# A state-space scan kernel: most of the step sizes' last additions and products moved from VectorE's step stage into the scan on GpSimd

## The chip, the cores and the metric

One core of a Trainium2 chip runs the whole program in one launch. The metric is the device time of one execution in microseconds (us), lower is better. The engines are TensorE (PE in the profile; its weight loads are PEld), VectorE (DVE), ScalarE (ACT), GpSimd (POOL) and SyncE (SP), which issues the DMAs. Each engine runs its own list of instructions in order and meets the others through semaphores.

## The reference, cut to what matters

The model is four small layers on an image of 2 x 32 x 32 tokens with 32 channels. The change lies in the first one, a selective scan over 8 x 8 windows in four directions (64 inner channels, 16 states):

```python
x_dbl = jnp.einsum('bkdl,kcd->bkcl', xs, x_proj_w)
dts, Bs, Cs = jnp.split(x_dbl, [DT_RANK, DT_RANK + D_STATE], axis=2)
dts = jnp.einsum('bkrl,kdr->bkdl', dts, dt_projs_w)
dts = jax.nn.softplus(dts + dt_projs_b[None, :, :, None])
...
def step(h, inp):
    u, dt, Bl, Cl = inp
    dA = jnp.exp(dt[..., None] * A)
    h = h * dA + (dt * u)[..., None] * Bl[:, :, None, :]
    y = jnp.einsum('bkdn,bkn->bkd', h, Cl)
    return (h, y)
```

What follows (the directions put back in order and added, a layer norm, a gate, an output projection, and then the layers with two recurrences of 1,024 steps, the experts and the attention) is computed as before and is not touched.

## The kernel before

The four directions are held as two pairs: `k` is the pair, the 128 partitions are 2 directions x 64 channels, and the free axis is 16 windows x 128 positions = 2,048 columns. So `step` (the step sizes dt), `drive` (dt times u) and `seqf` (u) are each 128 x 2 x 2,048 in f32.

The work is cut into blocks. At a block's end every engine waits for all the others. Around the change there are three:

- The token stage (lines 343 to 410) turns the convolved image into tokens and these into the four scan orders. ScalarE only copies every second pair of windows there.
- The step stage (lines 413 to 507) computes softplus(v) as max(v, 0) + ln(1 + exp(-|v|)) with a small correction of what the f32 addition 1 + exp loses. It goes by 8 chunks of 512 columns. TensorE makes v (line 432), ScalarE makes |v|, max(v, 0) (`above`) and the exponential (lines 446 to 449), VectorE makes the correction and adds it to `above` (lines 466, 473, 481) and cuts the B and C projections into three bf16 parts (lines 470 to 484). ScalarE then takes the 8 logarithms (line 457). At the end VectorE puts `step` together for 1,024 columns at a time, log minus `ln_one` plus `above` (line 495; `ln_one` is the logarithm of 1 as the engine computes it), four times, and makes the first two products `drive` = `step` x `seqf` (line 489). When the first logarithm is there, TensorE multiplies a constant tile 16 times for nothing (`keep_streaming`, line 95). A line of the profile with L95 is always such filling.
- The scan (lines 557 to 776) has 64 units `u`: four groups of 1,024 columns (`u // 16`: pair 0 first half, pair 0 second half, pair 1 first half, pair 1 second half), and in each 16 states. For a unit TensorE spreads B over the partitions into PSUM (`p_bb`, line 587) and C (`p_cb`, line 593), ScalarE makes the decays `d_a` = exp(step x A) (line 659) and copies C to SBUF (`cb`, line 665), VectorE multiplies `drive` with B (line 712) and runs the recurrence with one scan instruction into `hs` (line 723), GpSimd multiplies `hs` with C into `hc` (line 776), and TensorE adds `hc` over the states into `p_y` (line 562, eight products of 128 columns). In each fourth unit (`u % 4 == 3`) GpSimd makes the product with B instead of VectorE (`d_bu`, line 771), from a copy that ScalarE makes (line 670) of a spread by TensorE (line 615), issued three units ahead at `u % 4 == 0`.

`hs`, `cb` and `hc` are rings of three, so the scan of unit u waits for the GpSimd product of unit u - 3 (`hc`), and TensorE's list at unit u has `p_bb(u)`, `p_cb(u)`, the sum of unit u - 3, and only then `p_bb(u + 1)`. The order of everything is written out by hand. GpSimd makes the other two `drive` products in the scan, at units 2 and 18 (line 767).

## Time and profile before

| | us |
|---|---|
| median of 3 runs | 990.17 (988.23 to 991.03) |
| the profiled execution | 990.42 |
| its span, first to last instruction | 988.6 |
| step stage, first to last work | about 36.6 to 67.1 |
| scan, first work to last scan instruction's end | about 67.4 to 276.2 |

The timeline rows below give a start, a duration and then engine, line and operation, `out<-in`, shapes and a count; in brackets stands how long the engine had been idle and what ended that. Rows that run together (x2) have one duration for the whole. Where operations overlap in their pipeline, the step from one start to the next is a little shorter than a duration. In the rows of windows each engine has its busy time in that stretch with the number of instructions, and then come the granted TensorE clock (1.00 is 2.4 GHz, 0.50 is 1.2 GHz), the busy share of the DMA engines and GB/s.

### The profile page before, as it was taken

The numbers are of one execution on the slowest core, as the hardware profiler recorded it, in microseconds if no ns is written. First come the engines' busy times: TensorE is split into PE (matmuls) and PEld (weight loads), VectorE is DVE, ScalarE is ACT, GpSimd is POOL, SyncE is SP. The second block draws the span as 40 slices with busy tenths as digits, with TensorE's granted clock in tenths as the row PEclk, the third lists the DMA queues.
The fourth block names the chain that finished last, engine by engine and source line by source line (L and its number), as shares of the span: only waits on it lengthen the run. The fifth ranks groups of instructions, "written<-read, shape, count | busy, mean of one in ns | idle before, by whom it ended". The sixth has DMA issues, their size and how long they took to land. (4 is left out here: it accounts for less than half of the span.)

```text
span 988.6 us, 15415 instructions
## 1 busy us (share of the span) xinstructions
PE 905.6 (92%) x6234; PEld 517.4 (52%) x6234; DVE 417.7 (42%) x715; ACT 446.4 (45%) x1491; POOL 230.8 (23%) x140
## 2 busy tenths in 40 slices
PE   7848888888989988899999999999999999999986
PEld 4416667667764444344444444445555544554543
DVE  4599999999966654600000000002005400302653
ACT  4667777777635443233333333333333333334542
POOL 3209999899820000110000000000000000000410
PEclk9968999999999997999999999999999999999887
DMA  3020000000000000200000000000000000000000
GB/s 80 15 51 1 1 1 2 1 1 1 1 1 6 2 24 11 80 1 1 1 1 1 1 1 2 1 1 1 1 1 1 1 1 1 1 1 2 1 24 11
DMA packets 10320, 8.30 MB, mean 8 GB/s; under 512 B 7346, under 2 KB 8610, under 8 KB 10152
## 3 DMA queue, kind: packets, MB, share of 16 engines
q1 hardware_dynamic: 10248, 7.31, 3.0%
q8 instruction: 49, 0.80, 0.4%
q14 instruction: 23, 0.19, 0.1%
HBM read 5.47 MB, written 0.26 MB: 6 GB/s over the span
## 5 line engine op out<-in xcount | busy, mean ns | idle before, releaser
L895 PE MATMUL L2p_z<-stream 128*128 128x512 bf16 x943 | 366.8, 390 | 0.0
L937 ACT ACTIVATE L2yx<-L2p_z 32x2 f32<-32x2 f32 x1024 | 165.3, 161 | 323.0 <-PE L2p_z L914 323.0
L914 PEld LDWEIGHTS L2p_z<-L2yx,L2v 64*32 64x32 f32 x2048 | 137.6, 104 | 224.7 <-ACT L2yx L937 218.5
L914 PE MATMUL L2p_z<-L2yx,L2v 64*32 64x2 f32 x2048 | 225.5, 178 | 1.0 <-PEq L811 0.9
L776 POOL TENSOR_TENSOR hc<-hs,cb 128x1024 f32<-128x1024 f32 x64 | 149.7, 2360 | 11.6 <-DVE hs L723 11.5
L562 PEld LDWEIGHTS p_y<-ident,hc 128*128 128x128 f32 x1024 | 125.1, 193 | 10.3 <-POOL hc L776 1.1
L1602 DVE COPY xn<-L2yx 32x512 f32<-32x512 f32 (+1 forms) x2 | 0.8, 384 | 302.7 <-ACT L2yx L937 302.7
L562 PE MATMUL p_y<-ident,hc 128*128 128x128 f32 x1024 | 125.7, 277 | 0.0
L1602 POOL COPY xn<-L2yx 32x128 f32<-32x128 f32 x1 | 0.3, 284 | 484.0 <-SPq L1945 484.0
L723 DVE TENSOR_TENSOR_SCAN hs<-d_a,p_bb 128x1024 f32<-128x1024 f32 x48 | 109.8, 2287 | 6.6 <-ACT d_a L659 0.5
L895 PEld LDWEIGHTS L2p_z<-stream 128*128 128x128 bf16 x943 | 90.1, 96 | 15.1
L665 ACT ACTIVATE cb<-p_cb 128x1024 f32<-128x1024 f32 x64 | 65.3, 1020 | 10.8 <-PE p_cb L593 10.3
L659 ACT ACTIVATE d_a<-step,decay 128x1016 f32<-128x1016 f32 x48 | 54.6, 1138 | 19.7 <-DVE hs L723 12.8
L712 DVE TENSOR_TENSOR p_bb<-drive,p_bb 128x1024 f32<-128x1024 f32 x48 | 58.1, 1209 | 2.3 <-PE p_bb L587 2.2
L593 PE MATMUL p_cb<-c_parts,pick 96*128 96x512 bf16 x128 | 40.0, 395 | 12.3 <-ACT d_bu L670 10.5
L587 PE MATMUL p_bb<-b_parts,pick 96*128 96x512 bf16 x96 | 30.0, 395 | 13.1 <-DVE hs L723 7.2
L771 POOL TENSOR_TENSOR d_bu<-drive,d_bu 128x1024 f32<-128x1024 f32 x16 | 37.9, 2368 | 8.5 <-ACT d_bu L670 8.5
L723 DVE TENSOR_TENSOR_SCAN hs<-p_bb,d_bu 128x1024 f32<-128x1024 f32 x16 | 36.3, 2266 | 0.7 <-ACT p_bb L659 0.7
L593 PEld LDWEIGHTS p_cb<-c_parts,pick 96*128 96x128 bf16 x128 | 10.8, 99 | 31.0 <-ACT d_bu L670 18.8
L670 ACT ACTIVATE d_bu<-p_cb 128x1024 f32<-128x1024 f32 x16 | 16.4, 1024 | 18.8 <-PE p_cb L615 18.8
L1011 ACT ACTIVATE L0yx<-L0p_z 32x64 f32<-32x64 f32 x96 | 15.5, 209 | 14.3 <-PE L0p_z L988 14.3
L95 PE MATMUL L0p_fill<-stream 128*128 128x512 bf16 x56 | 20.6, 388 | 0.0
(513 smaller groups left out, 883.0 us busy)
## 6 DMA issues: line engine op xcount, KB each, us to landing
y_l<-in_pick SPq DMA_DIRECT2D x1, 768.0 KB
b_parts<-part SPq DMA_DIRECT2D x6, 128.0 KB, 2.3
c_parts<-part SPq DMA_DIRECT2D x6, 128.0 KB, 2.3
pos<-in_pos SPq DMA_DIRECT2D x1, 512.0 KB, 3.6
ao<-in_at_o SPq DMA_DIRECT2D x1, 512.0 KB, 4.1
L1w<-in_L_w SPq DMA_DIRECT2D x1, 297.0 KB
L3w<-in_L_w SPq DMA_DIRECT2D x1, 297.0 KB
x_tok<-in_x SPq DMA_DIRECT2D x2, 128.0 KB, 3.0
```

What stands on the lines that cost most here:

```text
L562: last = pe.matmul(p_y[:, j], hc[:, v % RING, j * L:(j + 1) * L], ident[:], start=False, stop=(v % NS == NS - 1 and j % 4 == 3))
L587: last = pe.matmul(p_bb[:, u % 2, h * BANK:(h + 1) * BANK], pick[:, n], b_parts[:, k, c], start=True, stop=True)
L593: last = pe.matmul(p_cb[:, h * BANK:(h + 1) * BANK], pick[:, n], c_parts[:, k, c], start=True, stop=True)
L659: act.activation(dst[:, :, 1:L], src[:, :, 1:L], ACT.Exp, scale=decay[:, k, n:n + 1]).then_inc(sig["d_a"], 1)
L665: act.activation(cb[:, u % RING], p_cb[:], ACT.Copy).then_inc(sig["p_cb_read"], 1)
L712: dve.tensor_tensor(p_bb[:, u % 2], drive[:, k, c0:c0 + UC], p_bb[:, u % 2], ALU.mult).then_inc(sig["d_bu"], 1)
L723: dve.tensor_tensor_scan(hs[:, u % RING], decays, inputs, 0.0, ALU.mult, ALU.add).then_inc(sig["scanned"], 1)
L771: pool.tensor_tensor(d_bu_of(u), drive[:, k, c0:c0 + UC], d_bu_of(u), ALU.mult).then_inc(sig["d_bu_pool"], 1)
L776: pool.tensor_tensor(hc[:, u % RING], hs[:, u % RING], cb[:, u % RING], ALU.mult).then_inc(sig["hc"], 1)
L895: pe.matmul(p_z[:, 1, 0:each], stream[:, 0:128], stream[:, 0:each], start=True, stop=True)
L914: pe.matmul(p_step[:, t % 2], v[:, 0:C], yx[:, NB * t:NB * (t + 1)], start=True, stop=True).then_inc(s("preact"), 1)
L937: act.activation(yx[0:C, NB * (t + 1):NB * (t + 2)], p_step[:, t % 2], ACT.Sigmoid).then_inc(s("state"), 1)
```

## The change

`ln_one` is now taken off where the correction is added to `above`, in each of the 8 chunks (a `scalar_tensor_tensor` in place of a `tensor_tensor`). What is left at the end is `step` = log + `above`. VectorE does that addition and the product for the first group of 1,024 columns alone. The other three additions and three products are GpSimd's in the scan: additions ahead of units 0, 18 and 34, products ahead of units 5, 22 and 38. `above` therefore outlives the step stage, and `y_tok` and `y_sq` use the room of `conv` and `tok`. ScalarE waits at units 16, 32 and 48 for the addition of the group that begins there.

`ln_one` is made in the token stage, and ScalarE loads the tables of its logarithm and then of its exponential there. At the start of the scan ScalarE makes the decays of units 0 and 1 before it copies C of unit 0, and TensorE fills with 4 idle products in each of units 0, 1 and 2. It fills with 18 instead of 16 in the step stage.

```diff
@@ -231,2 +231,4 @@
             pick = sb("pick", [96, NS, 128], BF16, stack=st)
+            above = sb("above", [128, 2, NW * L], stack=st)
+            ln_one = sb("ln_one", [128, 2], stack=st)
             tok = sb("tok", [L, NW, D], stack=st)
@@ -275,2 +277,3 @@
                             pool.memset(w_dt[:], 0.0)
+                            pool.memset(ln_one[:], 0.0)
                             pool.wait_ge(sig["load_in"], 64)
@@ -346,3 +349,2 @@
                     NPAIR = NW // 2
-                    ln_one = sb("ln_one", [128, 2], stack=s2)
                     with nc.Block() as block:
@@ -352,3 +354,2 @@
                             pool.tensor_copy(pick[:], pick_f)
-                            pool.memset(ln_one[:], 0.0)
                             pool.memset(zeros[:], 0.0)
@@ -406,2 +407,4 @@
                         def _(act):
+                            act.activation(ln_one[:, 0:1], ln_one[:, 0:1], ACT.Ln, bias=1.0)
+                            act.activation(ln_one[:, 1:2], ln_one[:, 1:2], ACT.Exp).then_inc(sig["ln_one"], 1)
                             for i in range(1, NPAIR, 2):
@@ -416,3 +419,2 @@
                     rest = sb("rest", [128, NW * L], stack=s3)
-                    above = sb("above", [128, 2, NW * L], stack=s3)
                     ex = sb("ex", [128, 2, NW * L], stack=s3)
@@ -437,3 +439,3 @@
                             pe.wait_ge(sig["log1"], 1)
-                            keep_streaming(pe, p_d[:, 0], 16)
+                            keep_streaming(pe, p_d[:, 0], 18)
 
@@ -441,3 +443,3 @@
                         def _(act):
-                            act.activation(ln_one[:, 1:2], ln_one[:, 1:2], ACT.Exp)
+                            act.wait_ge(sig["ln_one"], 1)
                             for i in range(NCH):
@@ -453,3 +455,2 @@
                             act.wait_ge(sig["exp_neg"], NCH)
-                            act.activation(ln_one[:, 0:1], ln_one[:, 0:1], ACT.Ln, bias=1.0)
                             for i in range(NCH):
@@ -480,3 +481,4 @@
                                     dve.wait_ge(sig["step_read"], i)
-                                    dve.tensor_tensor(above[:, k, c], above[:, k, c], drive[:, k, c], ALU.add).then_inc(sig["with_max"], 1)
+                                    dve.scalar_tensor_tensor(above[:, k, c], above[:, k, c], ln_one[:, 0:1], drive[:, k, c],
+                                                             ALU.subtract, ALU.add).then_inc(sig["with_max"], 1)
                                 if 1 <= i <= 4:
@@ -485,15 +487,8 @@
 
-                            def product(m):
-                                k, c = wide(m)
-                                dve.wait_ge(sig["softplus"], m + 1)
-                                dve.tensor_tensor(drive[:, k, c], step[:, k, c], seqf[:, k, c], ALU.mult)
-
                             dve.wait_ge(sig["with_max"], NCH)
-                            for m in range(4):
-                                k, c = wide(m)
-                                dve.wait_ge(sig["log1"], 2 * m + 2)
-                                dve.scalar_tensor_tensor(step[:, k, c], step[:, k, c], ln_one[:, 0:1], above[:, k, c],
-                                                         ALU.subtract, ALU.add).then_inc(sig["softplus"], 1)
-                                if m in (1, 2):
-                                    product(m - 1)
+                            k, c = wide(0)
+                            dve.wait_ge(sig["log1"], 2)
+                            dve.tensor_tensor(step[:, k, c], step[:, k, c], above[:, k, c], ALU.add).then_inc(sig["softplus"], 1)
+                            dve.wait_ge(sig["softplus"], 1)
+                            dve.tensor_tensor(drive[:, k, c], step[:, k, c], seqf[:, k, c], ALU.mult)
 
@@ -522,4 +517,4 @@
                 y_raw = sb("y_raw", [L, HW8, D], stack=s2)
-                y_tok = sb("y_tok", [L, NW, D], stack=s2)
-                y_sq = sb("y_sq", [L, NW, D], stack=s2)
+                y_tok = conv
+                y_sq = tok
                 stat = sb("stat", [L, 3, NW], stack=s2)
@@ -594,2 +589,4 @@
                                 last.then_inc(sig["p_cb_made"], 1)
+                                if u < RING:
+                                    keep_streaming(pe, p_y[:, 0:4].rearrange("p w d -> p (w d)"), 4)
                             if u == NU + RING - 2:
@@ -647,5 +644,6 @@
 
-                        act.wait_ge(sig["first_decay_zero"], 1)
-                        for u in range(NU):
+                        def decays(u):
                             k, c0, n = unit(u)
+                            if u and u % NS == 0:
+                                act.wait_ge(sig["softplus"], 1 + u // NS)
                             if u >= 2:
@@ -659,2 +657,9 @@
                             act.activation(dst[:, :, 1:L], src[:, :, 1:L], ACT.Exp, scale=decay[:, k, n:n + 1]).then_inc(sig["d_a"], 1)
+
+                        act.wait_ge(sig["first_decay_zero"], 1)
+                        decays(0)
+                        decays(1)
+                        for u in range(NU):
+                            if u >= 2:
+                                decays(u)
                             if u >= NS and u % NS == RING:
@@ -764,5 +769,11 @@
                         for u in range(NU):
-                            if u in (2, 2 + NS):
-                                c = slice(u // NS * UC, (u // NS + 1) * UC)
-                                pool.tensor_tensor(drive[:, 1, c], step[:, 1, c], seqf[:, 1, c], ALU.mult)
+                            if u in (0, 2 + NS, 2 + 2 * NS):
+                                k, c0, _ = unit(NS * (u // NS + 1))
+                                c = slice(c0, c0 + UC)
+                                pool.tensor_tensor(step[:, k, c], step[:, k, c], above[:, k, c], ALU.add).then_inc(sig["softplus"], 1)
+                            if u in (5, 6 + NS, 6 + 2 * NS):
+                                k, c0, _ = unit(NS * (u // NS + 1))
+                                c = slice(c0, c0 + UC)
+                                pool.wait_ge(sig["softplus"], u // NS + 2)
+                                pool.tensor_tensor(drive[:, k, c], step[:, k, c], seqf[:, k, c], ALU.mult)
                             if u % SHARE == 0:
```

The end of VectorE's list in the step stage and its first unit in the scan, before:

```order
L481 TENSOR_TENSOR above<-above,drive 128x512 [waits step_read,lost] x2
L495 SCALAR_TENSOR_TENSOR step<-step,ln_one,above 128x1024 [waits log1,with_max]
L495 SCALAR_TENSOR_TENSOR step<-step,ln_one,above 128x1024 [waits log1]
L489 TENSOR_TENSOR drive<-step,seq 128x1024 [waits softplus]
L495 SCALAR_TENSOR_TENSOR step<-step,ln_one,above 128x1024 [waits log1]
L489 TENSOR_TENSOR drive<-step,seq 128x1024 [waits softplus]
L495 SCALAR_TENSOR_TENSOR step<-step,ln_one,above 128x1024 [waits log1]
```

Of these four additions and two products one of each is left on VectorE:

```order
L482 SCALAR_TENSOR_TENSOR above<-above,ln_one,drive 128x512 [waits step_read,lost] x2
L491 TENSOR_TENSOR step<-step,above 128x1024 [waits log1,with_max]
L493 TENSOR_TENSOR drive<-step,seq 128x1024 [waits softplus]
L427 UNCONDITIONAL_BRANCH
L710 UNCONDITIONAL_BRANCH [waits barrier_Pool_Activation_PE_DVE_SP_release]
L717 TENSOR_TENSOR p_bb<-drive,p_bb 128x1024 [waits b_spread]
```

Three additions and one product left VectorE's list ahead of the end of the block.

GpSimd's list over the units 16 to 27 (`hc` is the product with C, `d_bu` the one with B of each fourth unit), before:

```order
L771 TENSOR_TENSOR d_bu<-drive,d_bu 128x1024 [waits p_cb_read]
L776 TENSOR_TENSOR hc<-hs,cb 128x1024 [waits y_summed,p_cb_read,scanned] x2
L767 TENSOR_TENSOR drive<-step,seq 128x1024
L776 TENSOR_TENSOR hc<-hs,cb 128x1024 [waits y_summed,p_cb_read,scanned] x2
L771 TENSOR_TENSOR d_bu<-drive,d_bu 128x1024 [waits p_cb_read]
L776 TENSOR_TENSOR hc<-hs,cb 128x1024 [waits y_summed,p_cb_read,scanned] x4
L771 TENSOR_TENSOR d_bu<-drive,d_bu 128x1024 [waits p_cb_read]
```

and now:

```order
L782 TENSOR_TENSOR d_bu<-drive,d_bu 128x1024 [waits p_cb_read]
L787 TENSOR_TENSOR hc<-hs,cb 128x1024 [waits y_summed,p_cb_read,scanned] x2
L773 TENSOR_TENSOR step<-step,above 128x1024
L787 TENSOR_TENSOR hc<-hs,cb 128x1024 [waits y_summed,p_cb_read,scanned] x2
L782 TENSOR_TENSOR d_bu<-drive,d_bu 128x1024 [waits p_cb_read]
L787 TENSOR_TENSOR hc<-hs,cb 128x1024 [waits y_summed,p_cb_read,scanned] x2
L778 TENSOR_TENSOR drive<-step,seq 128x1024 [waits softplus]
L787 TENSOR_TENSOR hc<-hs,cb 128x1024 [waits y_summed,p_cb_read,scanned] x2
L782 TENSOR_TENSOR d_bu<-drive,d_bu 128x1024 [waits p_cb_read]
```

An addition stands where the product stood, and four units later a product; the units 32 to 43 have the same pair, where there was none.

TensorE's list at the start of the scan, units 0 and 1, before:

```order
L587 MATMUL p_bb<-b_parts,pick 128x512 x2
L593 MATMUL p_cb<-c_parts,pick 128x512 x2
L615 MATMUL p_cb<-b_parts,pick 128x512 [waits p_cb_read]
L615 MATMUL p_cb<-b_parts,pick 128x512
L587 MATMUL p_bb<-b_parts,pick 128x512 x2
```

and now:

```order
L582 MATMUL p_bb<-b_parts,pick 128x512 x2
L588 MATMUL p_cb<-c_parts,pick 128x512 x2
L95 MATMUL p_y<-stream 128x512 x4
L612 MATMUL p_cb<-b_parts,pick 128x512 [waits p_cb_read]
L612 MATMUL p_cb<-b_parts,pick 128x512
L582 MATMUL p_bb<-b_parts,pick 128x512 x2
```

The 4 idle products stand ahead of the spread for unit 3 and of B for unit 1; at units 1 and 2 they stand behind `p_cb` too.

## Rows read from the trace of the kernel before

**Rows 1.** page, part 1, the whole program

```profile
PE 905.6 (92%) x6234; PEld 517.4 (52%) x6234; DVE 417.7 (42%) x715; ACT 446.4 (45%) x1491; POOL 230.8 (23%) x140
```

**Rows 2.** windows: busy us (instructions) of each engine, granted clock, DMA share, GB/s

```profile
60.00:62.00 2.00, 1.45 (x6) 0.43 (x4) 2.00 (x2) 0.60 (x2) 0.00 (x0) 0.94 0.00 0
62.00:64.00 2.00, 0.00 (x0) 0.00 (x0) 2.00 (x3) 0.00 (x0) 0.00 (x0) 0.91 0.00 0
...
66.00:80.00 14.00, 9.82 (x25) 3.65 (x26) 12.08 (x8) 9.93 (x11) 7.55 (x5) 0.50 0.00 0
80.00:81.00 1.00, 1.00 (x8) 1.00 (x7) 1.00 (x1) 0.64 (x1) 1.00 (x1) 0.65 0.00 0
...
120.00:200.00 80.00, 68.73 (x501) 55.15 (x499) 77.12 (x45) 59.28 (x65) 75.00 (x33) 1.00 0.00 1
```

**Rows 3.** timeline, step stage's end: start us, duration, engine, line, operation

```profile
55.51 5.94 PE L95 MATMUL p_d<-stream 128*128 128x512 bf16 x16 [6.97 <-ACT step L457]
...
59.96 2.48 DVE L495 SCALAR_TENSOR_TENSOR step<-step,ln_one,above 128x1024 f32<-128x1024 f32 x2
...
62.35 1.22 DVE L489 TENSOR_TENSOR drive<-step,seq 128x1024 f32<-128x1024 f32 x1
...
65.82 1.28 DVE L495 SCALAR_TENSOR_TENSOR step<-step,ln_one,above 128x1024 f32<-128x1024 f32 x1
...
67.42 1.01 PE L587 MATMUL p_bb<-b_parts,pick 96*128 96x512 bf16 x2 [5.97 <-PEq L425]
...
68.47 1.23 DVE L712 TENSOR_TENSOR p_bb<-drive,p_bb 128x1024 f32<-128x1024 f32 x1 [1.37 <-PE p_bb L587]
```

**Rows 4.** timeline, token stage and start of the step stage

```profile
30.54 0.59 ACT L388 COPY seq<-p_s 128x512 f32<-128x512 f32 x1 [4.68 <-PE p_s L383]
...
36.57 1.28 ACT L442 ACT_TABLE_LOAD   x1 [0.27 <-PEq L348]
...
36.61 1.10 PE L432 MATMUL p_d<-seq,w_dt 128*128 128x512 f32 x2 [0.94 <-PEq L348]
...
37.98 0.67 ACT L446 ACTIVATE ex<-p_d,b_dt 128x512 f32<-128x512 f32 x1
...
41.94 0.43 DVE L466 TENSOR_SCALAR drive<-ex 128x512 f32<-128x512 f32 x1 [1.01 <-ACT ex L449]
```

**Rows 5.** groups by form, step stage (36 to 68 us): busy us, mean ns

```profile
L481 DVE TENSOR_TENSOR above<-above,drive 128x512 f32<-128x512 f32 x8 | 5.4, 684 | 0.0
L495 DVE SCALAR_TENSOR_TENSOR step<-step,ln_one,above 128x1024 f32<-128x1024 f32 x4 | 5.0, 1280 | 0.0
```

**Rows 6.** timeline, VectorE in the undisturbed scan

```profile
105.46 2.27 DVE L723 TENSOR_TENSOR_SCAN hs<-p_bb,d_bu 128x1024 f32<-128x1024 f32 x1
107.64 1.21 DVE L712 TENSOR_TENSOR p_bb<-drive,p_bb 128x1024 f32<-128x1024 f32 x1
108.98 2.29 DVE L723 TENSOR_TENSOR_SCAN hs<-d_a,p_bb 128x1024 f32<-128x1024 f32 x1
```

**Rows 7.** timeline, GpSimd in the scan

```profile
118.43 4.68 POOL L776 TENSOR_TENSOR hc<-hs,cb 128x1024 f32<-128x1024 f32 x2 [1.16 <-DVE hs L723]
...
130.02 2.38 POOL L767 TENSOR_TENSOR drive<-step,seq 128x1024 f32<-128x1024 f32 x1
```

**Rows 8.** timeline, TensorE and VectorE in the first scan units

```profile
70.40 1.04 PE L615 MATMUL p_cb<-b_parts,pick 96*128 96x512 bf16 x2 [1.12 <-ACT cb L665]
...
72.33 1.23 DVE L712 TENSOR_TENSOR p_bb<-drive,p_bb 128x1024 f32<-128x1024 f32 x1 [0.24 <-PE p_bb L587]
...
82.00 1.23 DVE L712 TENSOR_TENSOR p_bb<-drive,p_bb 128x1024 f32<-128x1024 f32 x1 [0.35 <-PE p_bb L587]
```

**Rows 9.** timeline, TensorE at full clock in the scan

```profile
164.30 1.95 PE L562 MATMUL p_y<-ident,hc 128*128 128x128 f32 x16
...
172.74 0.59 PE L587 MATMUL p_bb<-b_parts,pick 96*128 96x512 bf16 x2
```

## The prediction, on record before the changed kernel ran

> **What bounds the kernel now.** I read the page's totals first [rows 1]: TensorE is busy for 92% of the span, but that is filling and the long recurrences behind the scan. The change touches none of that, so the totals don't price it. The windows [rows 2] do. From 120 to 200 us, in the scan, VectorE is busy 77.1 of 80 us and GpSimd 75.0: VectorE sets the pace and GpSimd has little left. From 62 to 66 us (one of the two windows is shown) VectorE alone works: TensorE, ScalarE, GpSimd and the DMAs stand at 0.00. So at the end of the step stage each microsecond taken off VectorE is one off the program, if nobody else ends later. The timeline of that end [rows 3] gives the pieces: additions from 59.96, the last ending at 65.82 + 1.28 = 67.10, TensorE's first scan matmul at 67.42 (0.32 for the change of blocks), VectorE's first product at 68.47.
>
> **VectorE's end of the step stage.** Before, 59.96 to 67.10 is 7.14 us: four additions and two products. Now it is one addition and one product. A two-input operation of 1,024 columns takes 1.22 (the product at 62.35) [rows 3]; the product reads what the addition just wrote, and such a pair has a gap of 108.98 - 107.64 - 1.21 = 0.13 [rows 6]. That is 1.22 + 0.13 + 1.22 = 2.57, so 4.57 less.
>
> The subtraction of `ln_one` moves into the 8 corrections. The three-input form takes 1,280 ns, against 1,220 of the two-input one, at 1,024 columns; the correction takes 684 ns at 512 [rows 3, 5]. The extra 0.06 may be a fixed cost (8 x 0.06 = 0.5) or go with the columns (8 x 0.03 = 0.24). I take 0.36. It counts in full, since VectorE has its last real wait of the stage at 41.94 [rows 4] and works from there to the end.
>
> The start of the stage moves the other way. The table load at 36.57 and its small operation make ScalarE start |v| at 37.98, while TensorE's product is there at 36.61 + 1.10 = 37.71 [rows 4]. Now ScalarE starts at about 37.75: 0.23 earlier, and VectorE's chain, which waited for ScalarE until 41.94, with it. The two loads in the token stage cost 2 x (1.28 + 0.2) = 3.0 us, in the 4.68 us in which ScalarE stood idle ahead of its first copy at 30.54 [rows 4]: nothing. (Past that cover, each further microsecond would delay the copy and the four pairs behind it.) Between exponentials and logarithms ScalarE loses only the small operation, 0.11, for which nobody waits.
>
> Sum of the stage: -4.57 + 0.36 - 0.23 = -4.44 us; VectorE ends at 62.66. With the two ends of the three-input price it is -4.3 to -4.56.
>
> Who could be late instead? ScalarE and the DMAs are at 0.00 from 62 us [rows 2]. TensorE now fills with 18 products from about 55.2. Before, 16 took 5.94, from 55.51 to 61.45 [rows 3]; the clock was 0.94 on average in 60 to 62 [rows 2], so half for 0.24 us and full after. With r for one at full and 2r at half clock, 4.73/2r + 1.21/r = 16, so r = 0.22. With the rise at the same moment, 18 end at about 61.7, before VectorE. If the clock rose in none of them, they would end at 55.2 + 18 x 0.45 = 63.3 and hold the block 0.6 us: the bound of this edit. At nothing, then.
>
> **The start of the scan.** Here the trace has the chip at half clock from 66 to 80 us, with the rise at about 80.7 (0.65 in 80 to 81) [rows 2], and TensorE is late for VectorE three times. A pair for `p_bb` takes 1.01 at half clock [rows 3] and 0.59 at full [rows 9]: 0.42 ahead of the first product. The second product comes 72.33 - 68.47 = 3.86 after the first, where an undisturbed unit takes 1.34 + 2.20 = 3.54 [rows 6, 8]: 0.32. The product of unit 4 comes at 82.00, 9.67 after that of unit 1, where 3.54 + 3.54 + 2.18 = 9.26 would do [rows 6, 8]: 0.41. In all 1.15 us to be had.
>
> Now TensorE stands idle for 62.98 - 61.7 = 1.3 us instead of 6, and then fills. What did the clock do? The last matmul ended at 61.45 and the clock fell inside 62 to 64 (0.91 is half for 0.36 us, so at 63.6) [rows 2], after 2.2 us of rest; it rose at 60.24, after 4.7 us of unbroken work. So it is likely, not certain, that 1.3 us of rest don't lose it. If it stays full: the first product 0.42 earlier; for unit 1 the bound is now ScalarE, which makes two decays (to 2.2 us after the block's start) before it copies C (to 3.2); the spread for unit 3 and `p_bb(1)` follow until 3.3 + 0.43 + 0.59 = 4.3, against 4.2 for which VectorE would ask: 0.15 lost instead of 0.32; unit 4 loses nothing. Gain 0.42 + 0.17 + 0.41 = 1.0. If it falls at 63.6 for some microseconds, `p_bb(0)` is just through, but four fillers at 0.45 and the spreads at half clock make `p_bb(1)` late by 0.5 instead of 0.32, and since TensorE now works without rest the clock is back before unit 4: 0.4 - 0.2 + 0.4 = 0.6. I take 0.7.
>
> The Trainium skill ("TensorE: Matmul & The Clock Gate", part 1, "What's actually happening") has the throttled clock as the default and activity as what releases it. By that alone the shorter rest keeps the clock and the sum would have 1.0 here; the row in which it fell after 2.2 us makes me stop at 0.7.
>
> **GpSimd.** Six additional operations stand where two stood: four more of 128x1024 at 2.38 each (the product at 130.02 [rows 7]; I take the addition to cost the same, as both read two tensors and write one), 9.5 us. The addition ahead of unit 0 runs from 0.2 to 2.6 us after the block's start, and the first `d_bu` must wait for a copy of the spread that started at 70.40, 3.0 us after it, and starts no earlier now [rows 3, 8]: free. The other pairs must fit into the idle time. Four units take 3 x 3.54 + 2.18 = 12.8 on VectorE [rows 6]; GpSimd has five operations of 2.33 from start to start, and the row at 118.43 shows what is left: 1.16 idle in each four units [rows 7]. An addition of 2.36 ahead of unit 18 eats the 1.16 and leaves GpSimd 1.2 late; the product ahead of unit 22 makes it 2.4 to 2.5; then it recovers 1.16 per four units and is on time again by unit 30. Units 34 and 38 repeat that; in the first group only the product at unit 5 stands in for the one at unit 2.
>
> Who waits meanwhile? The ring of three: scan 27 needs `hc(24)`. Normally `hc(24)` ends 3.65 us after scan 24, and scan 27 starts 3.54 + 3.54 + 2.18 - 2.27 = 7.0 after it: 3.35 spare, 0.9 with the delay. And TensorE: it adds `hc(24)` in 1.95 and makes `p_bb(28)` in 0.6 [rows 9] behind it, so at 3.65 + 2.5 + 2.55 = 8.7, and VectorE asks at 9.26: 0.56 spare. That is the tightest place, and it holds. ScalarE's new waits at units 16, 32 and 48 are for additions 14 to 16 units old. Cost nothing; its bound is the rival below.
>
> **The sum.** -4.44 - 0.7 = -5.1 us. On the profiled execution 990.42 - 5.1 = 985.3. That execution is 0.25 above the median of 990.17, so against the runs it is 985.0. I say 985.1. The forecast's own range, with both ends of the three-input price, 0.3 to 1.0 at the scan's start, and the spread of the three runs (2.8 us), is 983.3 to 987.0.
>
> **Rivals.**
> *GpSimd becomes the bound (slower).* The spare at `hc(24)` and `hc(40)` is 0.56. If the additions, or all GpSimd's operations, were some 5% dearer, five of them would take 12.3 of 12.8 and the delay would not be recovered before the next pair; then each extra operation is paid by VectorE through the ring. Price: four at 2.38 = 9.5, so 990.4 + 9.5 - 5.1 = 994.8. For it: 75.0 of 80 us busy [rows 2]. Against it: the product at 130.02 in the same place moved VectorE by nothing, and 1.16 is idle. The Trainium skill ("GPSIMD Engine Reference", section 4.1) advises against just this move, since two-input elementwise work is about twice as slow there; the trace agrees (2.38 against 1.22), but what counts is who waits. 7%.
> *The fillers hinder (no change).* If the clock stays at half through the first units in spite of the filling, the fillers are in the way: `p_bb(1)` comes 5.35 us after the block's start instead of 4.87, and the sum of unit 0 behind three sets of fillers ends near 16.4, so `p_bb(4)` at 17.3 instead of 14.5: 2.8 later. 990.4 - 4.4 + 2.8 = 988.8. For it: the clock was at half for 14 us here with TensorE busy 9.8 of them [rows 2]. Against it: it rose after 4.7 us of unbroken work, which there now is. 9%.
> *Another engine ends the block.* The fillers of the step stage at half clock throughout hold it by 0.6, and the scan then starts at half clock and gains nothing: -3.8, 986.6. 10%.
>
> **How the numbers follow.** Forecast 74%. About 0.3% (3 us) is what a measurement of this kernel can tell from no change, so faster means below 987.2. Nearly all of the forecast and most of the 986.6 rival lie there: 0.82. The 988.8 rival and the upper end of the others are no change: 0.12. Slower: 0.06. The range 983.3 to 988.4 leaves out the GpSimd rival and part of the filler rival.
>
> **What would show it.** In the profile after: VectorE's last operation of the step stage ends 4.2 to 4.6 us earlier; the first |v| starts within 0.1 of TensorE's first product; the corrections take 0.71 to 0.75 us; a granted clock of 1.00 by five microseconds into the scan; units 0 to 4 without a gap above 0.2 on VectorE; around units 22 to 30 and 38 to 46 GpSimd without idle time and VectorE still at 12.8 per four units; the scan 0.6 to 1.0 shorter. VectorE idle with `hc` as releaser near unit 27 or 43 would make the forecast wrong, and so would fillers that end after VectorE.

## The result and the profile after

The changed kernel takes 981.28 us (median of 4 runs, 980.51 to 983.18) against 989.38 (4 runs, 988.23 to 991.03): a ratio of 0.9918, 95% interval 0.9902 to 0.9935. It is faster, as forecast, but by 8.1 us instead of 5.1, and 981.28 lies below the range of 983.3 to 988.4. The profiled execution took 980.51 us with a span of 978.7, that is 9.9 less of span than before.

The table sets the two profiled executions side by side at the same events. The end is the end of VectorE's last operation.

| event | before, us | after, us | shift |
|---|---|---|---|
| VectorE's last operation of the step stage ends | 67.10 | 62.85 | -4.25 |
| its first product of the scan starts | 68.47 | 63.79 | -4.68 |
| its product of unit 4 starts | 82.00 | 76.72 | -5.28 |
| its last scan starts | 273.88 | 268.20 | -5.68 |
| the copies behind the next norm start | 299.68 | 292.86 | -6.82 |
| the second recurrence starts | 420.73 | 413.14 | -7.59 |
| the attention is over, last norm's copies start | 962.51 | 952.44 | -10.07 |
| VectorE's last operation ends | 984.83 | 974.92 | -9.91 |

The first four rows are the change. The rest is a stretch whose code is the same in both kernels, except that `y_tok` and `y_sq` lie in other room: from the last scan to the end it took 710.95 us before and 706.72 after. In that stretch the clock was at half for 47.4 us before and for 37.4 after.

The timeline of VectorE, ScalarE, TensorE and GpSimd at the end of the step stage and the scan's start, after (columns as in [rows 3]):

```profile
55.34 6.48 PE L95 MATMUL p_d<-stream 128*128 128x512 bf16 x18 [6.71 <-ACT step L458]
...
58.94 1.41 DVE L482 SCALAR_TENSOR_TENSOR above<-above,ln_one,drive 128x512 f32<-128x512 f32 x2
...
60.38 1.22 DVE L491 TENSOR_TENSOR step<-step,above 128x1024 f32<-128x1024 f32 x1
61.63 1.22 DVE L493 TENSOR_TENSOR drive<-step,seq 128x1024 f32<-128x1024 f32 x1
...
63.16 0.59 PE L582 MATMUL p_bb<-b_parts,pick 96*128 96x512 bf16 x2 [1.34 <-PEq L427]
63.18 2.37 POOL L773 TENSOR_TENSOR step<-step,above 128x1024 f32<-128x1024 f32 x1
...
63.79 1.23 DVE L717 TENSOR_TENSOR p_bb<-drive,p_bb 128x1024 f32<-128x1024 f32 x1 [0.93 <-PE p_bb L582]
```

One addition and one product are left, from 60.38 to 62.85. TensorE rests 1.34 us instead of 5.97 [rows 3], and its first pair takes 0.59 instead of 1.01. GpSimd's first addition runs while nothing waits for it. In the token stage ScalarE's two table loads end long ahead of its first copy, and it waits for TensorE's first product in the step stage:

```profile
27.70 1.28 ACT L409 ACT_TABLE_LOAD   x1
29.00 0.20 ACT L409 ACTIVATE ln_one<-ln_one 128x1 f32<-128x1 f32 x1
30.62 0.59 ACT L389 COPY seq<-p_s 128x512 f32<-128x512 f32 x1 [1.43 <-PE p_s L384]
...
37.90 0.69 ACT L448 ACTIVATE ex<-p_d,b_dt 128x512 f32<-128x512 f32 x1 [1.51 <-PE p_d L434]
```

The windows after, beside [rows 2]: none of the windows shown from 62 us on is at half clock, and GpSimd is now full.

```profile
60.00:62.00 2.00, 1.82 (x8) 0.64 (x6) 1.93 (x3) 0.43 (x2) 0.00 (x0) 0.93 0.00 0
...
66.00:80.00 14.00, 11.71 (x68) 6.98 (x69) 13.58 (x8) 10.59 (x12) 11.84 (x6) 1.00 0.00 0
120.00:200.00 80.00, 69.83 (x506) 55.72 (x504) 77.59 (x44) 59.95 (x66) 79.79 (x36) 1.00 0.00 1
```

GpSimd is busy 79.79 of 80 us where it was 75.0, and VectorE still does its work in them.

Behind the scan the largest part of the difference is the attention (53.66 us before, 51.18 after). The place that is easiest to read comes earlier. Between the two halves of the turned image TensorE rests 2.2 us in both kernels. Before, and the clock of that stretch:

```profile
284.49 1.15 PE L632 MATMUL p_bb<-ident,y_tok 64*64 64x64 f32 x32
285.57 1.25 PE L95 MATMUL p_y<-stream 128*128 128x512 bf16 x5
289.00 1.97 PE L632 MATMUL p_bb<-ident,y_tok 64*64 64x64 f32 x32 [2.18 <-DVE y_tok L740]
```

```profile
288.00:291.00 3.00, 2.00 (x33) 0.65 0.00 0
291.00:295.00 4.00, 4.00 (x10) 0.83 0.00 0
```

and after:

```profile
278.81 1.15 PE L629 MATMUL p_bb<-ident,conv 64*64 64x64 f32 x32
279.89 1.25 PE L95 MATMUL p_y<-stream 128*128 128x512 bf16 x5
283.32 1.15 PE L629 MATMUL p_bb<-ident,conv 64*64 64x64 f32 x32 [2.17 <-DVE conv L745]
```

```profile
282.00:285.00 3.00, 1.68 (x34) 1.00 0.00 0
285.00:289.00 4.00, 3.39 (x16) 1.00 0.00 0
```

The same work and the same rest, and the clock fell in one and not in the other. Where it fell, the second half took 1.97 us instead of 1.15, and the stretch from the last scan to the next norm 25.80 instead of 24.66.

### The profile page after: what moved, and what is told of

The parts are those of the page before. It is cut to its first block and busy times, and to the rows that moved or that the text cites. A ratio compares the mean times of both kernels' runs of the same rounds, so it can differ in the third digit from the quotient of the medians.

```text
span 978.7 us, 15448 instructions
## 1 busy us (share of the span) xinstructions
PE 900.6 (92%) x6248; PEld 514.2 (53%) x6248; DVE 414.0 (42%) x711; ACT 447.5 (46%) x1492; POOL 239.3 (24%) x144
## 5 line engine op out<-in xcount | busy, mean ns | idle before, releaser
L657 ACT ACTIVATE d_a<-step,decay 128x1016 f32<-128x1016 f32 x48 | 54.5, 1138 | 13.6 <-DVE hs L728 10.7
```

The source lines that it names most:

```text
L657: act.activation(dst[:, :, 1:L], src[:, :, 1:L], ACT.Exp, scale=decay[:, k, n:n + 1]).then_inc(sig["d_a"], 1)
```

## The experiments

"Five delays" and the like are idle VectorE products in scan units:

```diff
+                                if u in (9, 13, 28, 45, 57):
+                                    dve.tensor_tensor(scratch[:], drive[:, k, c0:c0 + UC], p_bb[:, u % 2], ALU.mult)
                                 dve.tensor_tensor(p_bb[:, u % 2], drive[:, k, c0:c0 + UC], p_bb[:, u % 2], ALU.mult)
```

Each puts off the next scan by 1.13 us. The fifth, at unit 57, is nearly all given back: without it scan 59 waits 0.71 us for ScalarE, and with it that wait is gone, with 0.2 us more at unit 62. In the profile after, and in a_delay5:

```profile
252.15 2.29 DVE L728 TENSOR_TENSOR_SCAN hs<-d_a,p_bb 128x1024 f32<-128x1024 f32 x1
255.15 2.29 DVE L728 TENSOR_TENSOR_SCAN hs<-p_bb,d_bu 128x1024 f32<-128x1024 f32 x1 [0.71 <-ACT p_bb L657]
```

```profile
257.68 2.29 DVE L731 TENSOR_TENSOR_SCAN hs<-d_a,p_bb 128x1024 f32<-128x1024 f32 x1
259.89 2.26 DVE L731 TENSOR_TENSOR_SCAN hs<-p_bb,d_bu 128x1024 f32<-128x1024 f32 x1
```

Five delays therefore move the last scan by 4.6 us and not by the 5.65 that the expectations below count with; three of them, at units 9, 28 and 45, move it by 3.4.

All means and medians below are over all runs of a kernel; the kernel before ran beside them (chip means 989.3, 990.0, 990.4 and 991.0 of 31, 34, 15 and 31 runs; medians 988.5 to 989.6). "Behind" is the time from the last scan's start to VectorE's last operation in the profile.

**b_delay1**: the kernel before, one delay (unit 9).

> The kernel before with one idle VectorE product of 128x1024 in scan unit 9, whose result nobody reads: 1.1 us more work on the path. Theory (clock alignment): the changed kernel's 8 us are 5.7 us of shorter step stage and scan, and the rest is that TensorE's work behind the scan stands at other instants against those at which the chip moves the clock, so that it falls in fewer of TensorE's short rests. Then any small shift can change the time behind the scan by microseconds, and this one may make the kernel FASTER in spite of added work: up to 4 us gained back, 985 to 988. Rival (the gain behind the scan belongs to the new code, its tiles or addresses): exactly +1.1, 990.5 against 989.4, and the time from the scan's end to the program's end as before, 712.5 us.

Measured: median 990.04, mean 990.32 of 10 runs, 1.1 above its neighbours' mean of 989.25; ratio 1.0014 (0.9983 to 1.0045). The average agrees with the rival's sum, give or take 1.8 us, and lies outside the theory's 985 to 988. The profile agrees with the theory: its span is 986.1, shorter than the 988.6 of before in spite of the added work, and behind took 707.05. One execution of the unchanged code behind the scan can be 3.9 us shorter than another.

**a_delay5**: the changed kernel, five delays.

> The changed kernel with five idle VectorE products in scan units 9, 13, 28, 45 and 57: 5 x 1.13 = 5.65 us, so that everything behind the scan stands at the instants where it stood in the kernel before (5.68 shorter). Theory (clock alignment): the stretch from the scan's end to the program's end goes back to its length of before, 4.2 us longer, the clock falls at 288 to 292 us as before, and the span is 978.7 + 5.65 + 4.2 = 988.6. Rival (the gain behind the scan belongs to the new code): 978.7 + 5.65 = 984.4 of span.

Measured: span 985.0, mean 988.52 of 10 runs, behind 708.52. Neither number came out: the theory said 988.6, and the rival, with the delays at the 4.6 us that they cost, 983.3. Two of its parts went back to their length of before (25.75 to the next norm, 53.66 in the attention), others didn't. The last scan started at 272.69, 1.2 us ahead of the 273.88 of before, so the work did not stand at the same place, and whether the same place would bring the same clock is not tested.

**a_delay2**: two delays (units 9 and 28).

> The changed kernel with two idle VectorE products in scan units 9 and 28: 2.3 us more on the path. Theory (clock alignment): the stretch behind the scan takes a third length, neither 702.5 nor 706.7 us by necessity; the span is 981.0 plus something between 0 and 5. Rival (belongs to the new code): 981.0 of span, the stretch behind the scan at 702.5.

Measured: span 984.6, mean 985.54, behind 709.41: a third length. (The expectation's 702.5 and 706.7 are a slip; the two known lengths are 706.72 and 710.95.) VectorE also lost 0.9 us beyond the delay ahead of unit 28, where the clock had fallen at 151.7, the first sight of what pool_close and after_third show.

Why these lengths differ can be seen in the windows around 51 to 54 us. The code to there is the same in all variants of the changed kernel and TensorE has been resting since about 48.6; yet the clock falls at another instant. In the second profile of the changed kernel, and in a_more:

```profile
51.00:51.50 0.50, 0.00 (x0) 0.71 0.00 0
53.00:53.50 0.50, 0.00 (x0) 0.50 0.00 0
```

```profile
51.00:51.50 0.50, 0.00 (x0) 1.00 0.00 0
53.00:53.50 0.50, 0.00 (x0) 1.00 0.00 0
53.50:54.00 0.50, 0.00 (x0) 0.83 0.00 0
```

It fell at 51.2 in one and at 53.8 in the other. Over the first ten profiles it lies between 51.0 and 53.8. So the instants at which the clock moves differ from run to run for the same code. With them differs the time at half clock behind the scan: 37.3 to 47.4 us in 17 profiles (all but a_more), and of two profiles the one with a microsecond more of it is longer there by about a third of one (correlation 0.86). That is why I take the clock for the cause of the differing lengths; no experiment sets the instants and shows it.

**stage_only**: neither fillers in the scan nor the new order of ScalarE, and 16 fillers in the step stage.

> The changed kernel without the scan's twelve fillers, with 16 fillers in the step stage, and with ScalarE's order of before (decays of unit 0, copy of C, then decays of unit 1). What is left is the move of additions and products and the tables. My sum has -4.4 us (measured -3.8 to -4.1 at the block's end) at the scan's first product and 0.6 to 1.0 from the fillers and the order, which is lost here: the first scan instruction 0.3 to 0.4 later than in the changed kernel against the block's start if the clock has fallen by then, the clock at half for ten or more microseconds of the scan as before, unit 4's product 0.8 us late in all. If instead the clock stays at full without the fillers, the scan starts as in the changed kernel and the fillers were worth nothing. Behind the scan it stands at yet another instant, so the total says little: 980 to 986.

```diff
-                                if u < RING:
-                                    keep_streaming(pe, p_y[:, 0:4].rearrange("p w d -> p (w d)"), 4)
...
-                        decays(0)
-                        decays(1)
                         for u in range(NU):
-                            if u >= 2:
-                                decays(u)
+                            decays(u)
```

Measured: mean 983.33 of 10 runs, ratio 0.9939 (0.9912 to 0.9966). The first product came at 64.05 and that of unit 4 at 77.1. The clock was at half from 65.5 to 75.7 us and cost 0.36 us ahead of unit 4. The mean is 5.9 below its neighbours' (give or take 1.5): most of the gain is the shortened step stage.

**after_again** and **after_third**: the changed kernel itself.

> The changed kernel once more, unchanged, with many runs on one chip beside those of the kernel before. What my steps give: 5.1 to 5.8 us of shorter step stage and scan. The stretch behind the scan had five different lengths in six profiles (706.7 to 711.0 us). Theory (clock alignment by chance): it is drawn anew in each run, so over many runs it cancels, and the difference of medians is 5 to 6.5 us, not 8.1: ratio near 0.994. Rival (a shift of 5.7 us lands well in every run): 8 us or more again, ratio 0.992.

> The changed kernel a third time, unchanged, for the size of the gain. So far 15 runs of it average 982.6 us, and the runs of the kernel before average 989.3 (31 on one chip) and 990.0 (34 on another): 7.0 less, where the step stage and the scan are shorter by 5.0 to 5.7 in the profiles. In every profile so far the clock falls at another instant (51.0 to 53.8 us) although the code to there is the same, so chance is in it. Theory (alignment is drawn anew each run): the gain comes out between 5 and 7, and the average over all three is nearer 6 than 8. Rival (a steady gain behind the scan): 7 to 8 again.

Measured: 982.70 median, 982.99 mean of 11 runs, ratio 0.9922 (0.9897 to 0.9947); and 983.26, 982.98 of 6 runs, ratio 0.9924 (0.9897 to 0.9951). With the first four, 21 runs average 982.7; 115 runs of the kernel before average 990.1. By these means the gain is 7.4 us, give or take 1.0 (7.0 and 7.4 against the neighbours on the same chip); by medians, 989.3 against 982.7, it is 6.6. The forecast's 5.1 lies outside that, the first 8.1 at its upper end. The last scan started at 268.8 and 269.8 in these profiles, against 268.2 in the first: the scan has losses that differ by run, too. In after_again the clock fell for some 3 us at the scan's start (0.65 lost at unit 2). In after_third it fell at 151.3 (0.76 lost at units 28 and 29) and again at 202.5:

```profile
202.28 3.60 PE L557 MATMUL p_y<-ident,hc 128*128 128x128 f32 x16 [1.82 <-POOL hc L787]
205.67 0.72 PE L582 MATMUL p_bb<-b_parts,pick 96*128 96x512 bf16 x2
```

```profile
203.28 2.26 DVE L728 TENSOR_TENSOR_SCAN hs<-p_bb,d_bu 128x1024 f32<-128x1024 f32 x1
206.43 1.23 DVE L717 TENSOR_TENSOR p_bb<-drive,p_bb 128x1024 f32<-128x1024 f32 x1 [0.89 <-PE p_bb L582]
```

TensorE waits 1.82 us for GpSimd's `hc(40)`, the clock falls 0.2 us behind the end of that rest, the sum takes 3.60 instead of 1.95 [rows 9], and VectorE waits 0.89 for `p_bb(44)`. In the first profile the same place, 16 units earlier, had a rest of 1.72 without a fall, and `p_bb(28)` was ready at 152.78, with VectorE's product at 153.57:

```profile
150.29 2.05 PE L557 MATMUL p_y<-ident,hc 128*128 128x128 f32 x16 [1.72 <-POOL hc L787]
152.18 0.60 PE L582 MATMUL p_bb<-b_parts,pick 96*128 96x512 bf16 x2
```

**start_only**: the kernel before with the new start of the scan alone.

> The kernel before with nothing changed but the scan's start: four fillers in each of units 0 to 2, and ScalarE's decays of units 0 and 1 ahead of the copy of C. TensorE still rests 6 us at the end of the step stage, so the scan starts at half clock. By my forecast's sum the fillers bring the clock back before unit 4 (0.4 us gained) and make unit 1 later (0.2 lost): first product as before (68.5), unit 4's product at 81.8 instead of 82.0, so -0.2 us. By the rival of my forecast (fillers hinder at half clock): unit 4's product 2.8 us later, at 84.8.

Measured: median 989.97, ratio 1.000 (0.998 to 1.002). First product at 68.86, unit 4's at 82.1, 13.2 us apart instead of 13.5. With the fillers the clock was full from 72.3 on instead of 80.7 us:

```profile
66.00:70.00 4.00, 2.19 (x6) 0.50 0.00 0
70.00:75.00 5.00, 4.43 (x16) 0.77 0.00 0
75.00:80.00 5.00, 4.49 (x28) 1.00 0.00 0
```

They cost 0.1 us at unit 1 and not the rival's 2.8, which ends that rival; without the shorter rest ahead of them they are worth nothing measurable. In this profile the clock fell once more at 92.8, and VectorE lost 1.13 us at unit 8.

**pool_close**: the second and third GpSimd product right behind their additions.

```diff
-                            if u in (5, 6 + NS, 6 + 2 * NS):
+                            if u in (5, 3 + NS, 3 + 2 * NS):
```

> The changed kernel with GpSimd's products of the second and third pair at units 19 and 35, one unit behind their additions, instead of 22 and 38. By my count of GpSimd's delay: it is 1.2 us late behind unit 18 and 3.5 us late behind unit 19 (before any idle time comes). hc(20) then ends 3.65 + 3.5 = 7.2 us after scan 20, with 7.0 until scan 23 must start and 9.26 until p_bb(24) is wanted, for which TensorE needs 2.55 behind it: 0.5 late. So VectorE should lose 0.2 to 0.6 us near unit 23 or 24 and again near 39 or 40, about 1 us in all, where the changed kernel loses none. If GpSimd is not near its bound (margins larger than I counted): no loss at all. If it is the bound: 2.4 us at each place.

Measured: mean 986.22, 3.2 above after_again on the same chip (give or take 2.0). In the profile VectorE lost 2.0 us at units 23 to 25 and 0.47 at 39 and 40, 2.5 in all, where I expected about 1. At the first place the clock fell as well, at 140.3 (0.57 in the last window):

```profile
138.00:140.00 2.00, 0.65 (x5) 1.00 0.00 0
140.00:142.00 2.00, 2.00 (x13) 0.57 0.00 0
```

At the second it held, and 0.47 lies within my 0.2 to 0.6. So my count of GpSimd's delay holds there: a product moved by three units is enough to reach VectorE.

**a_wide**: the three products four units later; the delay of GpSimd stays at 1.2 us.

```diff
-                            if u in (5, 6 + NS, 6 + 2 * NS):
+                            if u in (9, 10 + NS, 10 + 2 * NS):
```

> The changed kernel with GpSimd's three products four units later, at units 9, 26 and 42 instead of 5, 22 and 38, so that GpSimd is never more than about 1.2 us late (2.5 before). Then TensorE has no rest of 1.7 us ahead of the sum of unit 24, in which the clock fell in one run of the changed kernel with a delay. Theory: VectorE loses nothing in the profile, as in the changed kernel, and on average over runs 0 to 1 us is gained, 982 to 983. Rival (the margin never mattered): the same as the changed kernel within 0.5 us. If a later product comes too late for its group: several us slower.

Measured: mean 981.86 of 6 runs beside 982.98 of after_third, and 983.12 of 8 on another chip (aw_again, below). No loss at units 27 and 43 in either profile, nor in those of a_wide_tail, aw_delay3 and aw_delay5: behind the scan's start the clock fell in none of these five scans, while with the products at 22 and 38 it fell in 3 of 8 (after_third, a_delay2, a_nofill). The gain in time is within the scatter.

**a_wide_tail**: a_wide with 12 fillers between the halves of the turned image instead of 5.

> a_wide with 12 instead of 5 idle TensorE products between the two halves of the turned image, the one filling of a_more that stands in a rest of 2.2 us and kept no one waiting there. The stretch from the last scan to the next norm took 24.7 us where the clock held and 25.8 where it fell, in 5 of 10 profiles each. Theory: 24.7 in nearly every run, 0.5 us less on average than a_wide. Rival: the fillers cost as much as they save, same as a_wide within 0.5 us.

Measured: mean 981.98 of 6 runs, as a_wide; the stretch to the next norm at 24.66 in its one profile. Not told apart.

**a_more**: more fillers at four places behind the scan.

> The changed kernel with more idle TensorE products behind the scan, in places where the trace has it resting: 12 instead of 5 between the two halves of the turned image, 29 instead of 24 and 6 additional ones in each of the two expert layers, 3 ahead of the attention's first norm. Theory (the time behind the scan is set by whether the clock falls in those rests): the clock falls less often, the stretch behind the scan comes below 706 us and is less scattered; gain of 1 to 4 us over the changed kernel, 978 to 982. Rival (the fillers only get in the way of what comes next on TensorE, or the clock falls elsewhere): within 1 us of the changed kernel, or slower by up to 1 us.

Measured: mean 986.86 of 12 runs, 3.9 slower than after_again. The rival was right and too mild. The attention took 54.22 us and what follows it 25.28, where after_again has 51.41 and 22.24. The additional fillers of the last expert layer keep TensorE longer. Here, and in after_again:

```profile
958.81 7.88 PE L95 MATMUL L3p_t<-stream 128*128 128x512 bf16 x28
```

```profile
955.92 6.94 PE L95 MATMUL L3p_t<-stream 128*128 128x512 bf16 x24
```

Both met half clock for some 3 us. That accounts for 0.9 of the 5.9 us; the longer attention is no sure effect of the fillers, since it took 53.7 in three kernels without them. Where the rest comes from stays open.

**a_nofill**: the changed kernel without the twelve fillers.

> The changed kernel without the twelve fillers at the scan's start, with all else of it kept (decays first, 18 fillers in the step stage). By my forecast they are in the way at half clock and help to keep or regain full clock. In stage_only (neither fillers nor order) the clock was at half from 68 to 78 us and VectorE lost 0.3 at unit 3, where the changed kernel lost 0.2 at unit 0. So: first products within 0.3 us of the changed kernel, a stretch at half clock between 65 and 80 us, 0.1 to 0.5 us lost before unit 8; total within 1 us of the changed kernel.

Measured: median 984.96, mean 985.70 of 8 runs (one of 992.4), 1.7 above after_third by medians and 2.7 by means (give or take 2.6). The clock fell behind the scan's start, from 67.6 to 77.8, and VectorE lost 1.5 us ahead of unit 4:

```profile
74.62 2.26 DVE L726 TENSOR_TENSOR_SCAN hs<-p_bb,d_bu 128x1024 f32<-128x1024 f32 x1
78.34 1.23 DVE L715 TENSOR_TENSOR p_bb<-drive,p_bb 128x1024 f32<-128x1024 f32 x1 [1.45 <-PE p_bb L582]
```

So the fillers can be worth more than the 0.1 to 0.5 us that I expected, in runs in which the clock falls there; in stage_only, also without them, the same fall cost 0.36. The 1.7 us are not theirs alone, since this profile also lost 1.7 at units 28, 29 and 44, as after_third did. What they do shows in the clock: in the two profiles without them it stayed at half for some 10 us, in the five profiles with them in which it fell there, for some 3.

**aw_again, aw_delay5, aw_delay3, b_delay5**: is the rest of the gain a matter of place?

> a_wide once more, as the reference of this set: 982 us, no loss near units 27 and 43 on VectorE.

> a_wide with five idle VectorE products (5.65 us), so that the work behind the scan stands about where it stands in the kernel before. Theory (place matters on average): the average is 6.5 to 8 us above aw_again, near 989. Rival (chance in the sample): 5.4 to 6.2 us above it, 987.6.

> a_wide with three idle VectorE products (3.4 us). Theory (place matters on average): the average differs from aw_again + 3.4 by up to 2 us to either side. Rival (chance): 3.2 to 3.9 us above aw_again.

> The kernel before with the same five idle products. Both theories have it 5.65 us above the kernel before if the place does not matter; if place matters on average, its distance to the kernel before differs from 5.65 by more than 1 us, to either side. Rival of both (the gain behind the scan belongs to the new code): aw_delay5 stays 7 us below this kernel, as the changed kernel below the one before.

| kernel | runs | mean | median | last scan moved by the delays |
|---|---|---|---|---|
| aw_again | 8 | 983.1 | 982.5 | 0 |
| aw_delay3 | 12 | 985.7 | 984.9 | 3.4 |
| aw_delay5 | 12 | 989.1 | 989.1 | 4.6 |
| kernel before | 31 | 991.0 | 989.6 | 0 |
| b_delay5 | 12 | 995.0 | 994.6 | 4.6 |

By means the delays cost 2.5 and 6.0 in the changed code and 4.1 in the old one, each give or take some 2 us. These differ from 3.4 and 4.6 by 0.5 to 1.4, on both sides. Place does not show, and none of these rules out that it matters by a microsecond or two. The new code at the same delay stays 5.9 below the old, give or take 2.0, which does not tell 5.9 from 7.

## Why the prediction was wrong

**The end of the step stage: right, a little less.** I had VectorE's end at 62.66; it was 62.85, and 62.9 on average over 13 profiles. The addition and the product took 2.47 (60.38 to 62.85) where I had 2.57: the gap of 0.13 between them was 0.03. The three-input form is a fixed 0.06 dearer in each of the eight chunks (the pair at 58.94 took 1.41, the same pair before 1.29), 0.5 us in all: the upper of my two ends. ScalarE starts |v| 0.08 us earlier (37.90 against 37.98) and not 0.23; half of what is missing is that the whole program stood 0.08 us later. Fillers end at 61.82, before VectorE.

**The start of the scan: right where the clock held.** The forecast had 1.0 with the clock held and 0.6 with a fall, and I took 0.7. The first profile held it: -4.25 at the block's end became -5.28 at unit 4, 1.0. In after_again it fell, unit 4 stands 13.6 us behind the first product instead of 12.9, and the gain to there is 0.4. Of twelve profiles with this start behind the shorter rest, the clock held in seven and fell in five. The new order of ScalarE costs 0.16 at unit 1, as counted.

**GpSimd: right, and as tight as said.** Six operations cost VectorE nothing in the first profile; the spare that I put at 0.56 us was 0.79. pool_close shows that one step tighter costs 0.5 where the clock holds and 2.0 where it falls. What I missed is that TensorE now rests 1.7 to 1.8 us ahead of the sum at this spot, that in some runs the clock falls within a microsecond or so behind that rest, and that the sum then takes up to 3.60 instead of 1.95 and uses up the spare. The price of the GpSimd rival, 9.5 us, was too high by its own numbers: with some 0.5 us still idle in each four units, most of the four operations would have been made up for.

**The sum of these steps** was -5.1. Up to the last scan's start the first profile has -5.68; 0.36 of that is a single late scan of unit 33 in the profile of before, which came back in start_only and not in b_delay1. The old code loses time to the clock in the scan as well: three of its profiles have the last scan at 273.9, 274.1 (b_delay1) and 275.7 (b_delay5), delays taken off. Six profiles of the changed code have it at 268.1 to 269.8. By the averages it is 5.9: about 4.3 at the end of the step stage and 1.5 to 1.6 behind it, where I had 0.7.

**The step that failed** is the sentence that the change touches nothing of the filling and the long recurrences behind the scan, which put that stretch at nothing in the sum, and the range that followed from it. The work there is untouched, but its length is not a constant: between the two profiles it shrank by 4.2 of the 9.9 us, and in 17 profiles (a_more aside; a_wide_tail has seven more fillers there) it took 706.7 to 711.0, longer where the clock was at half for longer. The attention took 51.2 to 51.4 us in 14 of them and 53.7 in three, and the profile of before is one of the three. On average over the profiles the stretch is as long in the new code as in the old (708.0 over 13 profiles and 708.3 over 4, known to about a microsecond), so the 4.2 were largely the luck of this pair. I took the scatter of three runs (2.8 us) for the scatter of the kernel; 31 runs of it on one chip lie between 983.1 and 996.3. The median of four runs, 981.28, was lucky too, but luck is not all: the mean of 21 runs, 982.7, also lies below my 983.3, and the second term that was too small is the one for the scan, about 1.5 instead of 0.7.

**What stays open.** Of the 7.4 us between the means about 5.9 are in the step stage and the scan and 0.3 behind it. The rest, about a microsecond, isn't settled and is about as large as the uncertainty of the means. Part of it is in runs of which there is no profile: 19 of the 115 runs of before took over 993 us, and 1 of the 21 of the changed kernel over 987. The clock alone does not explain those, for 11 of the 19 had a mean granted clock of 0.962 or more, as the runs at 988 to 991 had. A cause in the new code behind the scan wasn't found, and the other room of `y_tok` and `y_sq` was not tested by itself.

## What to carry to other kernels

Operations that end a stage alone on one engine are worth their full time, and the engine that paces the next stage is not the one to ask whether they fit there: count the idle time of the engine that takes them in per period, then follow its lateness through the ring to the engine behind. Space such operations so that the lateness of one is gone before the next comes; the spare can be smaller than one trace shows, because behind a rest that it causes on TensorE the clock fell in some runs. Where an idle operation is put in as a delay, measure what it moves: one of the five here stood ahead of a wait and moved almost nothing. And before a range is set, ask how much the untouched part differs between runs; three runs don't tell.

## What the runs showed of the hardware

The granted clock fell at instants between 51.0 and 53.9 us in 18 profiles, with the same work on TensorE up to there and TensorE resting in all of them since 48.4 to 49.0. A rest of 1.82 us in the scan was followed by a fall 0.2 us behind its end in one run (after_third), while rests of 1.83 us ahead of other sums and one of 2.17 us behind the scan were not. Where the clock fell at the scan's start in spite of the shorter rest ahead of it, it was back after some 3 us where TensorE had idle products to fill with (five profiles) and after some 10 us where it had none (stage_only, a_nofill). Idle products at full clock in the scan's first units kept no one waiting (first profile); 28 of them in the last expert layer, for 3 us of that at half clock, took 7.88 us, ahead of real work.
